# First graph layer rebuilt: paired and merged sorted rows, part of the node rows picked by matmul instead of gathered

## The chip, the cores and the metric

One core of one Trainium2 chip runs the whole kernel. The metric is device time in microseconds (us) from start to end of one execution; lower is better. Engines are named as the profile names them: PE is TensorE (PEld its weight loads), DVE is VectorE, ACT is ScalarE, POOL is GpSimd, SP is SyncE.

## The reference, cut to what matters

```python
N, E, D = 8192, 262144, 128        # nodes, edges, features; dst is sorted, src is random
def layer0(x, src, dst, w, W):     # sums over edges into node src, reads node dst
    pre = segment_sum(x[dst] * w[:, None], src, N)
    return pre @ W.T
def layer1(x, src, dst, attr, ws): # tensor product with 9 attributes, reads src, sums into dst
    return segment_sum(tensor_product(x[src], attr, ws), dst, N) / sqrt(10)
x = layernorm(x + layer0(x, src, dst, edge_weight, W))
x = layernorm(x + layer1(x, src, dst, edge_attr_9, ws))
# dst = floor(8192 * u**2) for uniform u, then sorted; src uniform in 0..8191
```

Only the first layer and its preparation change. Its edges are given in order of dst, but their sums go to src, so both a gather (x[dst]) and a scatter-add (into src) are needed.

## The kernel before, in words

All edges are laid out as 128 rows of 2048, one row per SBUF partition. Five stages follow each other, each in a block of its own, with no overlap between blocks.

**setup** loads src, dst and weight as rows, builds a sort key (dst, and src above it) per edge on DVE, turns rows into columns with 32 PE transposes and ACT copies for the second layer's tables, and clears the accumulator `acc` (features on partitions, nodes along the free axis) on POOL (L220).

**sort_rows** sorts each partition's 2048 keys by src with a merge network of 66 stages on DVE: max, is_gt, min, and two predicated copies that carry the weight (L406 to L414), with ACT copying two halves per stage (L393, L395). Afterwards, element k of every partition has a src near the same place, so a tile of 128 edges, one from each partition, falls in a narrow window of src.

**layer0** loops over 128 rows of 16 tiles (2048 tiles of 128 edges). For each tile POOL gathers 128 rows of x from HBM by an indirect DMA (L525, into `l_feat`, two rows deep, 32 tiles); DVE makes a weighted one-hot of 704 columns (L631: `iota` equals `src_rel`, times `w_row`, eight buffers, `iota` in PSUM); PE multiplies the gathered rows by it in float32, as 512 and 192 columns (L567), adding 16 tiles up in PSUM; then DVE adds the row's 704 columns to `acc` at a window start read from memory (L641). Hand-over is by quads of four tiles: `hot_made` tells PE that four one-hots are there, `quad_done` tells DVE and POOL that PE is done with a quad. Ahead of its first one-hot DVE also makes the tables of the second layer (`layer1_tables`, L588 to L621).

**norm_stage** multiplies the sums by W and normalizes. **layer1** gathers again, 2048 times (L908), makes one-hots of 16 columns times nine attributes, and is not touched by the change; neither is the last **norm_stage**.

What sets the order around the change is the written order on each engine's queue and its semaphore waits; no planner is involved. A few lines of the old loop:

```python
dve.wait_ge(quad_done, u * (R // Q) + (R // Q + q + 3))      # quads up to two back are done
for t in range(Q * q, Q * q + Q):
    last = nc.vector.tensor_scalar(onehot[t % HOTS][:], iota[:, 0:WIN0], g.src_rel[:, col],
                                   g.w_row[:, col], ALU.is_equal, ALU.mult)
last.then_inc(hot_made, 1)
```

## Time and profile before

| what | value |
|---|---|
| median of 3 runs | 6743.53 us (6739.63 to 6747.98) |
| the profiled execution's own time | 6679.32 us |
| its span, first to last instruction | 6677.5 us |
| mean granted TensorE clock | 0.788 of full speed |
| busy: PE, PEld, DVE, ACT, POOL | 4653.5, 3185.8, 3323.1, 513.6, 3885.2 us |
| gathers | 4096, half of them in the first layer |

The profiled execution was shorter than the median of the timed runs by 64 us. Busy time counts compute and the POOL's making of DMA descriptors; register, branch and semaphore instructions are not counted. In the table by stage below, the columns are: stretch and its length in us; busy us (and instructions) of PE, PEld, DVE, ACT and POOL; granted TensorE clock; DMA share; GB/s. In the groups by line, busy us and mean ns stand ahead of the idle time before them and what ended it. A wait put down to "remote" has no releasing instruction in the records (some matmul records are missing).

### The profile page before, as it was taken

The page shows a single profiled execution, that of the slowest core. Times are in us where ns is not written, and L with a number is a line of the kernel's source. Part 1 is how long each engine was busy: PE and PEld are TensorE (multiplying, and loading weights), DVE is VectorE, ACT ScalarE, POOL GpSimd, SP SyncE. Part 2 cuts the span into 40 slices and gives each one's busy share as a digit, 9 for nine tenths or more (in the row PEclk, how much of TensorE's full clock was granted, in tenths as well). Part 3 has the DMA queues.
Part 4 walks back from the last instruction along what each step waited for, and adds up shares of the span by engine and source line. Part 5 has one row for each costly group of instructions (what it writes and reads, how often), then busy time and mean ns, then how long its engine had stood idle before and what let it go on. Part 6 is the DMA issues. An engine that isn't in the chain of part 4 may idle for free. (4 is left out here: it accounts for less than half of the span.)

```text
span 6677.5 us, 67026 instructions
## 1 busy us (share of the span) xinstructions
PE 4653.5 (70%) x16530; PEld 3185.8 (48%) x16531; DVE 3323.1 (50%) x4111; ACT 513.6 (8%) x954; POOL 3885.2 (58%) x4117
## 2 busy tenths in 40 slices
PE   0018888888888888888886666666666666676665
PEld 0004445544444454555455545555555555554454
DVE  9986666666666666666663222222222222222224
ACT  3320000000000000000002000000000000000002
POOL 0026666666666666666654666666666666666663
PEclk5559999999999999999995677776666767656666
DMA  0001111111111111111112111111111111111112
GB/s 22 0 13 44 44 44 44 45 44 44 45 45 44 44 44 45 44 44 45 44 36 83 47 47 47 47 47 47 47 47 47 47 47 47 47 47 47 47 47 78
DMA packets 145732, 298.91 MB, mean 45 GB/s; under 512 B 69280, under 2 KB 69408, under 8 KB 145328
## 3 DMA queue, kind: packets, MB, share of 16 engines
q0 software_dynamic: 131072, 268.70, 15.7%
q1 hardware_dynamic: 10032, 21.62, 1.1%
q10 hardware_dynamic: 4608, 8.39, 0.3%
q14 instruction: 15, 0.12, 0.0%
q8 instruction: 5, 0.08, 0.0%
HBM read 290.04 MB, written 8.39 MB: 45 GB/s over the span
## 5 line engine op out<-in xcount | busy, mean ns | idle before, releaser
L567 PE MATMUL l_pre<-onehot,l_feat 128*128 128x512 f32 (+1 forms) x8192 | 2610.1, 480 | 442.9 <-DVE onehot L631 427.5
L525 POOL DMA_INDIRECT l_feat<-in_x,l_ids x2048 | 1935.1, 945 | 1529.1 <-issue 1059.1
L908 POOL DMA_INDIRECT feat<-x,ids x2048 | 1934.0, 944 | 1124.2 <-issue 584.2
L631 DVE TENSOR_SCALAR onehot<-iota,src_rel,w_row 128x704 f32<-128x704 f32 x2048 | 1918.3, 1004 | 1007.1 <-remote 603.4
L567 PEld LDWEIGHTS l_pre<-onehot,l_feat 128*128 128x128 f32 x8192 | 1510.2, 198 | 1542.5 <-issue 1150.5
L1014 DVE TENSOR_TENSOR group<-group,quad 128x504 f32 (+1 forms) x512 | 347.2, 678 | 2186.0 <-PE quad L972 1115.2
L972 PE MATMUL quad<-attr_hot,feat 128*128 128x144 f32 x4096 | 1000.8, 399 | 559.9 <-issue 558.5
L972 PEld LDWEIGHTS quad<-attr_hot,feat 128*128 128x128 f32 x4096 | 833.6, 275 | 816.7 <-issue 816.1
L979 PE MATMUL mixed<-group,mix 128*128 128x192 f32 x2304 | 649.2, 463 | 333.3 <-DVE group L1014 223.0
L979 PEld LDWEIGHTS mixed<-group,mix 128*128 128x128 f32 x2304 | 607.5, 287 | 368.3 <-DVE group L1014 245.0
L964 PE MATMUL quad<-zero_bf 1*128 1x504 bf16 x512 | 248.6, 486 | 186.7 <-issue 186.4
L1000 DVE TENSOR_TENSOR attr_hot<-hot,attr_t 128x1152 f32<-128x1152 f32 x256 | 346.8, 1355 | 46.7 <-issue 20.2
L457 PE MATMUL turned<-cst,edge 128*128 128x128 f32 x2 | 0.7, 449 | 417.8 <-DVE edge L433 417.8
L549 ACT COPY l_ids<-gather_id 128x8 int32 x256 | 50.5, 197 | 2967.7 <-DMA l_feat<-in_x,l_ids 2943.8
L932 ACT CAST ids<-src_col 128x8 int32 x256 | 50.5, 197 | 2656.9 <-DMA feat<-x,ids 2591.7
L928 ACT ACTIVATE group<-group 128x1728 uint32<-128x1728 uint32 x128 | 210.3, 1643 | 131.5 <-remote 130.2
L457 PEld LDWEIGHTS turned<-cst,edge 128*128 128x128 f32 x2 | 0.3, 204 | 417.9 <-DVE edge L433 417.9
L948 PE MATMUL attr_t<-cst,attr_in 16*128 16x16 f32 x1161 | 154.4, 263 | 14.7 <-DMA attr_in<-in_edge_attr 14.4
L948 PEld LDWEIGHTS attr_t<-cst,attr_in 16*128 16x128 f32 x1161 | 142.0, 203 | 47.6 <-issue 47.6
L964 PEld LDWEIGHTS quad<-zero_bf 1*128 1x128 bf16 x512 | 59.4, 116 | 218.4 <-issue 203.9
L641 DVE TENSOR_TENSOR acc<-acc,l_pre 128x704 f32 x128 | 112.5, 879 | 5.8 <-PE l_pre L567 5.8
L414 DVE COPY_PREDICATED w_row<-swap,w_low 128x512 f32<-128x512 int32 (+9 forms) x66 | 98.0, 1484 | 2.3
(110 smaller groups left out, 904.8 us busy)
## 6 DMA issues: line engine op xcount, KB each, us to landing
l_feat<-in_x,l_ids POOLq DMA_INDIRECT x2048
feat<-x,ids POOLq DMA_INDIRECT x2048
attr_in<-in_edge_attr SPq DMA_DIRECT2D x129, 72.0 KB
norm_x<-in_x SPq DMA_DIRECT2D x16, 256.0 KB, 2.7
x<-norm_z ACTq DMA_DIRECT2D x16, 256.0 KB, 2.4
norm_x<-x SPq DMA_DIRECT2D x16, 256.0 KB, 2.7
out<-norm_z ACTq DMA_DIRECT2D x16, 256.0 KB, 2.4
rows_i<-in_src SPq DMA_DIRECT2D x1, 1024.0 KB, 6.0
```

Of the source, the lines that this page charges most:

```text
L525: pool.indirect_dma_start(feat[z][:, t, :], None, x, bass.IndirectOffsetOnAxis(ap=ids[z][t // H][:, t % H:t % H + 1], axis=0),).then_inc(f ...
L567: last = nc.tensor.matmul(pre[z][:, a:b], feat[z][:, t, :], onehot[t % HOTS][:, a:b], start=(t == 0), stop=(t == R - 1))
L631: last = nc.vector.tensor_scalar(onehot[t % HOTS][:], iota[:, 0:WIN0], g.src_rel[:, col], g.w_row[:, col], ALU.is_equal, ALU.mult)
L641: nc.vector.tensor_tensor(to, to, pre[z][:, 0:WIN0], ALU.add).then_inc(chunk_added, 1)
L908: pool.indirect_dma_start(feat[:, t, :], None, x1, bass.IndirectOffsetOnAxis(ap=ids[t // H][:, t % H:t % H + 1], axis=0),).then_inc(feat_i ...
L928: nc.scalar.memzero(group[z][:]).then_inc(group_zero, 1)
L948: last = nc.tensor.transpose(attr_t[:, z, m * R:(m + 1) * R], edges[:, :, m], g.cst[0:R, C_IDENT:C_IDENT + R])
L964: nc.tensor.matmul(quad[:, q, 0:NA * QUAD_WIN], zero_bf[0:1, 0:P], zero_bf[0:1, :], start=True, stop=False, skip_group_check=True)
L972: nc.tensor.matmul(bank[:, :, bass.ds(off, WIN)], feat[:, t, :], attr_hot[t // H][:, t % H, :, :], start=False, stop=(t % Q == Q - 1), ski ...
L979: last = nc.tensor.matmul(mixed[:, z, 0:GROUP_WIN], g.mix[:, m, :], group[z][:, m, :], start=(m == 0), stop=(m == NA - 1))
L1000: nc.vector.tensor_tensor(attr_hot[h][:], hot[:].unsqueeze(2).to_broadcast(s4), by_tile[:, h * H:h * H + H, :].unsqueeze(3).to_broadcast(s ...
L1014: nc.vector.tensor_tensor(to, to, quad[:, q, 0:NA * QUAD_WIN].rearrange("p (m n) -> p m n", m=NA), ALU.add).then_inc(quad_added, 1)
```

## The change

Rows r and 127-r are put on neighbouring partitions ("lanes" of a pair; `C_ROW`, `C_TURN`). With dst spread as the square of u, such a pair always covers about 128 different values of dst. Each lane is sorted as before, one of the two with its sign turned; the two lanes are then merged: they are exchanged by DMA (`far_keys`, `far_w`), compared once over 2048 elements, and run through four further stages (`blocks`). Now each pair holds 4096 edges in order of src, in 32 tiles of 128 edges that lie along the free axis; weights, dst and relative src are turned into columns by 48 PE transposes and 24 ACT copies.

A tile is now one pair's, so its src window is 360 columns (not 704), and its dst are within 160 nodes. Tiles are worked in groups of eight (256 groups). Of each eight, five are gathered (`GATHERS`) and three are picked (`FETCHED`): the pair's 160 nodes of x lie in SBUF, 128 of them split into three bfloat16 parts (`x_near`), the other 32 as three parts on spare partitions (`x_rest`). PE spreads the dst positions (`spread`, 3 bfloat16 matmuls a group), ACT and DVE make two 128-column one-hots a tile from them (`rest`, `near`), and PE picks the rows in four bfloat16 matmuls a tile (`fetch`); ACT copies them to SBUF (`message`). All eight tiles then go through one float32 matmul of 360 columns each into a PSUM window at an address read from memory (`pe_places`), 64 tiles added up in three banks, which DVE adds to `acc` (`adds`, 3 times 512 columns in every eight groups). POOL makes `x_near` and `x_rest` in six batches (8 gathers, 8 small operations each) beside the sort. The one-hots' `iota` is now in SBUF (it was in PSUM), the one-hot buffers are 16, the gather buffers 20. The rows of setup are loaded by three indirect DMAs on POOL, ahead of the clearing of `acc`; the tables of the second layer move from layer0 into setup.

The diff, cut to its core:

```diff
-WIN0 = 704
+WIN0 = 360
+BANKS = 3
+STEP = 512 - WIN0
+GROUP = 8
+FETCHED = (0, 3, 6)
+GATHERS = (1, 2, 4, 5, 7)
+KIND = (0, 2, 1, 0, 2, 1, 0, 1)
+FEATS = 20
+SUMMED0 = 18
+SPAN = 160
...
         def _(pool):                                    # setup
+            pool.wait_ge(row_no_made, 1)
+            pool.sem_inc(pool_turn, 1)
+            for k, (to, row) in enumerate(((rows_i[0], src), (rows_i[1], dst), (g.w_row, weight))):
+                pool.indirect_dma_start(to[:], None, row.rearrange("(r c) -> r c", r=RN),
+                                        bass.IndirectOffsetOnAxis(ap=row_no[:], axis=0)).then_inc(rows_in[k], 16)
             nc.gpsimd.memset(g.acc[:], 0.0)
...
+            link(nc.vector.tensor_reduce(lanes[:, 0, 0:1], rows_f[1][:], AX_X, ALU.min))
+            link(nc.vector.tensor_reduce(lanes[:, 0, 1:2], rows_f[1][:], AX_X, ALU.max))
...
+            layer1_tables(dve)
...
+    blocks = [(d, d) for d in (n // 2, n // 4, n // 8, P)]
...
+                if s == n_sort:
+                    dve.sem_inc(lanes_sorted, 1)
+                    dve.wait_ge(far_in, 64)
+                    nc.vector.scalar_tensor_tensor(swap[:], far_keys[:], -1.0, g.keys[:], ALU.mult,
+                                                   ALU.is_lt).then_inc(compared, 1)
+                    dve.wait_ge(compared, s + 1)
+                    nc.vector.scalar_tensor_tensor(g.keys[:], far_keys[:], -1.0, g.keys[:], ALU.mult, ALU.min)
+                    nc.vector.copy_predicated(g.w_row[:], swap[:], far_w[:]).then_inc(merged, 1)
...
+            def near(k, z):                              # DVE
+                dve.wait_ge(copied, k + 2)
+                dve.wait_ge(got_made, k + 1)
+                nc.vector.tensor_scalar(near_hot[z][:], place[z][:], wanted, None, ALU.is_equal).then_inc(near_made, 1)
+            def hots(k, h, s, j):
+                dve.wait_ge(staged, h * 3 + 3)
+                dve.wait_ge(summed, k * 2 + (SUMMED0 - 2))
+                for i in range(GROUP):
+                    c = j * GROUP + i
+                    made = nc.vector.tensor_scalar(hot_of[(j % 2) * GROUP + i], iota[KIND[i]], src_of[s][:, c:c + 1],
+                                                   w_of[s][:, c:c + 1], ALU.is_equal, ALU.mult)
+                    if i % 4 == 3:
+                        made.then_inc(hot_made, 1)
...
+            def rest(k, z):                              # ACT
+                act.wait_ge(placed, k + 1)
+                act.wait_ge(near_made, k + 1)
+                nc.scalar.copy(place[z][:], place_b[:, 0:NF * P]).then_inc(copied, 1)
...
+                nc.scalar.activation(rest_far[:], place[z][:], ACT.Abs, bias=not_wanted).then_inc(far_made, 1)
+                act.wait_ge(far_made, k + 1)
+                act.wait_ge(got_made, k + 1)
+                nc.scalar.activation(rest_hot[z][:], rest_far[:], ACT.Relu, bias=1.0, scale=-1.0).then_inc(rest_made, 1)
+            def message(k, z):
+                act.wait_ge(got_made, k + 3)
+                act.wait_ge(summed, k * 2 + (SUMMED0 - 2))
+                nc.scalar.copy(msg[z][:].rearrange("p a b -> p (a b)"), got[:, 0:NF * P]).then_inc(msg_made, 1)
...
+            for b in range(BATCHES):                     # POOL, beside the sort
+                for c, rows, landed in ((1, rest_in, rest_here), (0, near_rows, near_in)):
+                    for i in range(GATHERED):
+                        pool.indirect_dma_start(rows[:, i, :], None, x, ...).then_inc(landed, 16)
+                nc.gpsimd.tensor_copy(part, rest_in[:]).then_inc(pool_split, 1)
+                nc.gpsimd.tensor_tensor(rest_left[:], rest_in[:], part, ALU.subtract).then_inc(pool_split, 1)
...
+                                pool.wait_ge(summed, k * 2 + (SUMMED0 - 2 * (FEATS // NG) + 2))
+                                for m, i in enumerate(GATHERS):
+                                    pool.indirect_dma_start(feat[:, slot, :], None, x, ...).then_inc(feat_in[slot], 16)
...
+            def fetch(k, j):                             # PE
+                pe.wait_ge(near_made, k + 3)
+                pe.wait_ge(rest_made, k + 3)
+                pe.wait_ge(msg_made, k + 1)
+                for m in range(NF):
+                    for part in range(3):
+                        nc.tensor.matmul(to, near_hot[z][:, m * P:(m + 1) * P], x_near[:, a, part, :],
+                                         start=(part == 0), stop=False)
+                    last = nc.tensor.matmul(to, rest_hot[z][:, m * P:(m + 1) * P], x_rest[:, a, :], start=False,
+                                            stop=True)
+                last.then_inc(got_made, 1)
+            def sums(k, w, t, s, j):
+                places = pe_places(t, s, j)              # eight window starts read into registers
...
+                    made = nc.tensor.matmul(pre[:, s, bass.ds(places[i], WIN0)], rows, hot_of[(j % 2) * GROUP + i],
+                                            start=False, stop=(j == GROUPS - 1 and i == GROUP - 1),
+                                            skip_group_check=True)
+                    if i % 4 == 3:
+                        made.then_inc(summed, 1)
...
+                    def slots(t, final):                 # PE's order, group by group
+                                    spread(k + 2, ...)
+                                    fetch(k + 1, (j + 1) % GROUPS)
+                                sums(k, w, t, s, j)
```

The diff's calls are shortened where `...` stands inside a line, and `slots` is shown without its loop heads. DVE's order per group is near(k+2), hots(k+1), and in one group of eight adds; ACT's is rest(k+2), message(k+1).

## Rows read from the trace of the kernel before

**Rows 1.** Page, part 1: busy us and share of the span, whole kernel.
```profile
PE 4653.5 (70%) x16530; PEld 3185.8 (48%) x16531; DVE 3323.1 (50%) x4111; ACT 513.6 (8%) x954; POOL 3885.2 (58%) x4117
```

**Rows 2.** Busy time by stage: sort, layer0, layer1.
```profile
31.00:457.00 426.00, 1.70 (x6) 1.22 (x6) 408.64 (x350) 128.97 (x137) 0.00 (x0) 0.50 0.00 0
457.00:3504.00 3047.00, 2609.83 (x8192) 1510.23 (x8192) 2027.26 (x2190) 50.55 (x256) 1935.11 (x2048) 0.95 0.17 44
...
3563.00:6604.00 3041.00, 1966.44 (x8026) 1612.99 (x8027) 782.60 (x1145) 259.80 (x383) 1930.19 (x2044) 0.68 0.18 47
```

**Rows 3.** Groups of instructions by line, 457 to 3504 us (layer0).
```profile
L567 PE MATMUL l_pre<-onehot,l_feat 128*128 128x512 f32 (+1 forms) x8192 | 2610.1, 480 | 442.9 <-DVE onehot L631 427.5 <-issue 14.7
L525 POOL DMA_INDIRECT l_feat<-in_x,l_ids x2048 | 1935.1, 945 | 1529.1 <-issue 1059.1 <-PE l_pre L567 248.1 <-remote 221.9
```

**Rows 4.** Timeline of POOL in mid layer0: start, us, instruction, [idle before it].
```profile
2022.58 0.94 POOL L525 DMA_INDIRECT l_feat<-in_x,l_ids  x1 [3.06 <-PE l_pre L567]
```

**Rows 5.** Timeline of POOL while DVE makes the second layer's tables.
```profile
469.51 1.18 POOL L525 DMA_INDIRECT l_feat<-in_x,l_ids  x1 [0.30 <-issue]
...
472.25 1.38 POOL L525 DMA_INDIRECT l_feat<-in_x,l_ids  x1 [0.30 <-issue]
473.93 2.72 POOL L525 DMA_INDIRECT l_feat<-in_x,l_ids  x1 [0.30 <-issue]
```

**Rows 6.** Timeline of DVE at the end of layer0, when the gathers are over.
```profile
3485.46 3.77 DVE L631 TENSOR_SCALAR onehot<-iota,src_rel,w_row 128x704 f32<-128x704 f32 x4 [0.97 <-PE l_pre L567]
...
3490.19 3.77 DVE L631 TENSOR_SCALAR onehot<-iota,src_rel,w_row 128x704 f32<-128x704 f32 x4 [0.17 <-PE l_pre L567]
```

**Rows 7.** Timeline of DVE, the tables of the second layer, to its first one-hots.
```profile
463.98 0.46 DVE L588 TENSOR_TENSOR mix<-w_scalar,cst 128x288 f32<-128x288 f32 x1 [9.26 <-issue]
...
465.39 1.75 DVE L612 TENSOR_TENSOR off_f<-tile_start 128x1536 f32<-128x1536 f32 x1
...
469.40 0.48 DVE L607 TENSOR_SCALAR tile_offs<-word_f,keep 128x512 int32<-128x512 f32 x1
469.92 1.07 DVE L615 TENSOR_TENSOR off_f<-tile_start 128x512 f32<-128x512 f32 x1
...
472.19 1.32 DVE L618 TENSOR_SCALAR off_f<-tile_start,keep 128x2048 f32<-128x2048 f32 x1
473.54 2.29 DVE L619 TENSOR_TENSOR dst_rel<-dst_col,off_f 128x2048 f32<-128x2048 f32 x1
...
477.45 2.85 DVE L631 TENSOR_SCALAR onehot<-iota,src_rel,w_row 128x704 f32<-128x704 f32 x3 [1.18 <-issue]
```

**Rows 8.** Timeline of DVE in mid layer0, at the same place as POOL's.
```profile
2021.93 7.44 DVE L631 TENSOR_SCALAR onehot<-iota,src_rel,w_row 128x704 f32<-128x704 f32 x8 [5.00 <-remote]
```

**Rows 9.** Timeline of PE in setup: bfloat16 matmuls of 128 columns.
```profile
20.06 0.22 PE L299 MATMUL pt<-ident_bf,dst_lo 128*128 128x128 bf16 x1
20.11 0.22 PE L299 MATMUL pt<-ident_bf,dst_hi 128*128 128x128 bf16 x1
```

**Rows 10.** Timeline of a late sort stage, what follows the sort, ACT's 704 columns.
```profile
425.06 1.23 DVE L412 COPY_PREDICATED w_row<-swap,w_row 128x1020 f32<-128x1020 int32 x1
...
444.71 1.16 DVE L428 TENSOR_SCALAR src_i<-keys 128x2048 int32<-128x2048 int32 x1
...
455.07 0.75 ACT L537 COPY iota<-cst 128x704 f32<-128x704 f32 x1 [14.04 <-PEq L343]
```

**Rows 11.** Timeline of setup: clearing of acc, first cast of rows, a wait for ACT.
```profile
0.75 7.51 POOL L220 MEMSET acc<- 128x8896 f32 x1 [0.29 <-POOLq L1065]
...
7.64 1.76 DVE L236 CAST rows_f<-rows_i 128x2048 f32<-128x2048 int32 x1
...
24.28 0.18 DVE L263 COPY src_col<-src_col 128x16 f32<-128x16 f32 x1 [3.14 <-ACT tile_start L319]
```

**Rows 12.** Page, part 6: the load of the weights: count, KB, us to landing.
```profile
w_row<-in_edge_weight SPq DMA_DIRECT2D x1, 1024.0 KB, 10.0
```

**Rows 13.** Page, part 5: PE weight load behind a window start read from memory (layer1).
```profile
L964 PEld LDWEIGHTS quad<-zero_bf 1*128 1x128 bf16 x512 | 59.4, 116 | 218.4 <-issue 203.9
```

More of the change, by code:

```diff
@@ L165, in set_passes, with setup @@
     nc.vector.tensor_scalar(g.n_pass[:, layer:layer + 1], on, float(passes - 1), 1.0, ALU.mult, ALU.add)
-def setup(nc, g, src, dst, weight, w_lin, consts):
+def setup(nc, g, src, dst, weight, w_lin, w_tp, consts):
     RN, TN = g.RN, g.TN
@@ L188, in setup @@
         some = sb("some", [P, 4], F32)
+        g.tile_start = sb("tile_start", [P, TN], F32)
+        row_no = sb("row_no", [P, 1], I32)
+        turn_bf = sb("turn_bf", [P, P], BF16)
+        lanes = sb("lanes", [P, 2, 2], F32)
+        extent = sb("extent", [P, 2], F32)
+        lower = sb("lower", [P, 2], F32)
+        upper = sb("upper", [P, 2], F32)
+        keep_a = sb("keep_a", [P, 1], F32)
+        shown_in = sb("shown_in", [P, 3, PAIRS], F32)
+        w_scalar = sb("w_scalar", [P, MUL], F32)
+        w_vec = [sb(f"w_vec{i}", [P, MUL], F32) for i in range(2)]
+        off_f = sb("off_f", [P, TN], F32)
+        word_f = sb("word_f", [P, TN // QUAD_TILES], F32)
         some1 = sb("some1", [P, 1], F32)
@@ new lines, in _ @@
+            link(nc.vector.scalar_tensor_tensor(lower[:], lower[:], g.cst[:, C_UPPER:C_UPPER + 1], own,
+                                                ALU.mult, ALU.add))
+            link(nc.vector.tensor_tensor(upper[:], own, other, ALU.add))
+            link(nc.vector.tensor_tensor(upper[:], upper[:], lower[:], ALU.subtract))
+            link(nc.vector.tensor_tensor(extent[:, 1:2], lower[:, 1:2], upper[:, 0:1], ALU.subtract))
+            link(nc.vector.tensor_scalar(extent[:, 1:2], extent[:, 1:2], 0.5, None, ALU.is_gt))
@@ new lines, in _ @@
+            dve.wait_ge(miss_sum, 1)
+            link(nc.vector.tensor_scalar(some[:], pa[:, 0, 0:4], 0.5, None, ALU.is_gt))
+            link(nc.vector.tensor_reduce(some1[:], some[:, 1:4], AX_X, ALU.max))
+            set_passes(nc, g, 1, WIN, g.PASSES1, some1[:])
+            nc.vector.tensor_copy(g.on[:, 0:1], some[:, 0:1])
+            link(nc.vector.tensor_scalar(keep_a[:], some[:, 0:1], -1.0, 1.0, ALU.mult, ALU.add))
+            nc.vector.tensor_copy(g.pair[:, 1:2], upper[:, 0:1])
+            link(nc.vector.tensor_tensor(g.pair[:, 0:1], lower[:, 0:1], keep_a[:], ALU.mult))
@@ new lines, in _ @@
+            link(nc.vector.tensor_tensor(g.pair[:, 2:3], upper[:, 0:1], lower[:, 1:2], ALU.subtract))
+            link(nc.vector.tensor_scalar(g.pair[:, 2:3], g.pair[:, 2:3], 1.0, keep_a[:], ALU.subtract, ALU.mult))
+            link(nc.vector.tensor_tensor(g.pair[:, 3:4], lower[:, 1:2], lower[:, 0:1], ALU.subtract))
+            link(nc.vector.tensor_scalar(g.pair[:, 3:4], g.pair[:, 3:4], 1.0, None, ALU.add))
+            for k, col in enumerate((3, 0, 2)):
+                link(nc.vector.tensor_scalar(shown_in[:, k, :], g.cst[:, C_IDENT:C_IDENT + P:2],
+                                             g.pair[:, col:col + 1], None, ALU.mult))
@@ new lines, in _ @@
+        @block.scalar
+        def _(act):
+            cols = [g.src_col, g.dst_col]
+            for n in range(n_groups):
+                if n < len(col_groups):
+                    which, q = col_groups[n]
+                    dest = cols[which]
+                else:
+                    q, dest = n - len(col_groups), g.tile_start
+                act.wait_ge(group_done, n + 1)
+                o = dest[:, 0:TN].rearrange("p (r k) -> p k r", k=ROW_TILES)[:, 4 * q:4 * q + 4, :]
+                i = pt[:, n % 4, :].rearrange("p (j r) -> p j r", j=4)[:, :, 0:RN]
+                nc.scalar.copy(o, i).then_inc(group_out, 1)
+            act.wait_ge(wt_done, 1)
+            nc.scalar.copy(g.w_t[:], pa[:, 1, 0:P])
```

987 lines of the change are left out of this document (629 added, 358 removed).

## The prediction, made before the changed kernel was run

> **What bounds the kernel now.** I read the busy shares first [rows 1]: no engine is above 70%, so no engine bounds the whole. The table by stage [rows 2] says more: the span is a preparation of 457 us, layer0 of 3047 us, a norm to 3563, layer1 of 3041 us and a last norm. The preparation is DVE's (409 of 426 us busy in the sort). layer0 has PE 86% busy at a granted clock of 0.95, almost all of it the upper level, 2.4 GHz, after a sort at 0.50, 1.2 GHz, in which PE did nothing. layer1 has 2044 gathers in 3041 us and isn't touched; I leave its time as it is.
>
> Next, the groups of layer0 [rows 3]. PE idles 443 us, 428 of them until one-hots come; DVE idles 3047 - 2027 = 1020 us [rows 2], POOL 248 + 222 = 470 us besides its issue gaps. Each waits for the others. Their floors: POOL needs 0.94 + 0.30 = 1.25 us a gather (they start that far apart) [rows 4, 5], 16 x 1.25 = 20.0 us a row of tiles, 2560 us in all. PE, when gathers are long over and DVE follows it step by step, starts a quad every 3490.19 - 3485.46 = 4.73 us [rows 6], 18.9 us a row. Real pace: from the first one-hot at 477.45 [rows 7] to the end at 3504 is 3027 us with the last addition, 23.6 us a row, 1.18 times POOL's floor and 1.25 times PE's. The excess is hand-over: DVE stands 5.0 us ahead of eight one-hots, until a release that the records don't show [rows 8], and POOL 3.06 us until PE frees its buffer, at nearly the same moment [rows 4].
>
> The chain of waits that the page shows reaches back only through the last norm, so I go by the stages.
>
> **The loop after, per group of eight tiles (256 groups).**
>
> POOL: five gathers, 5 x 1.25 = 6.25 us, 1600 us in all, against 2560.
>
> PE: 704 columns took 4.73 / 4 = 1.18 us, so 360 take 0.605 us, and eight 4.84 us. The pick adds 3 + 12 bfloat16 matmuls of 128 columns with their weight loads; the rows show such pairs 0.055 us apart at the upper clock [rows 9]: 0.83 us. Three clearing matmuls in eight groups add about 0.1. Sum 5.8 us, 1480 us in all.
>
> DVE: a 704-column one-hot comes every 3.77 / 4 = 0.94 us [rows 6]. One column costs (2.29 - 1.75) / 512 = 1.05 ns [rows 7], so 360 columns take 0.94 - 0.36 = 0.58 us at this rate. But `iota` moves from PSUM to SBUF, and a one-source float32 operation from SBUF ran at double rate: 2048 elements in 1.32 us against 2.29 us for two sources [rows 7]. That takes 0.19 off: 0.39 us. I take 0.39 (0.58 is the bound). Eight are 3.15 us, `near` over 384 columns at most 0.48 [rows 7], I take 0.35, and three additions of 512 columns at 0.69 (2.29 less 1536 columns) in eight groups 0.26: 3.8 us (5.3 at the slow rate). DVE is covered by POOL either way.
>
> ACT: three operations over 384 columns and a copy of 384, each below the 0.75 us of 704 columns [rows 10]: under 3 us, covered too.
>
> What isn't free is DVE's double rate. Beside the tables the gathers got longer [rows 5]: 1.18 us beside a 0.48 us operation, 1.38 beside the 1.32 us one, 2.72 beside a two-source one of 2.29 us. The first of these ended 0.82 us after the DVE operation (469.88 to 470.69), the last also (475.83 to 476.65); the middle one ended 0.12 us after it. So I read a gather as two short accesses, near its start and at its end, each of which may have to wait for the DVE operation of the moment, and can slip in between two. With operations of 0.39 to 0.44 us an access waits at most that, half on the mean, and 3.5 of some 7 us of a group are such operations: 5 gathers x 2 x 0.2 x 0.5 = 1 us at most; I take 0.65, so POOL needs 6.9 us. Bounds: 0 and all of 3.5.
>
> The Trainium skill, SBUF — State Buffer, "Who interferes with whom", says that such a DVE operation holds the port pair that GpSimd needs for its whole length and that the other blocks fully. The middle and last gathers agree, but no row shows a train of such operations, where the question is who gets in between; if nobody does, the sum is 9.75 us a group instead of 7.4, the rival below.
>
> Pace: the old loop ran 1.18 times the floor of its slowest engine. 6.25 x 1.18 = 7.4; with 6.9 as the floor that leaves 0.5 for hand-over, less than before, but each hand-over is now per eight tiles, not four, and POOL is four groups ahead. I take 7.4 us: 256 x 7.4 = 1894 us, and 6.6 to 8.2 as this case's own range. PE is then busy 5.8 of 7.4 us in short gaps, 78%, between layer0's 86% at clock 0.95 and layer1's 65% at 0.68 [rows 2]. I take the upper level; at the lower level everywhere the matmuls would take 11.6 us, but PE would then never stop.
>
> **The preparation after.**
>
> Setup. The clearing of `acc` (7.51 us, from 0.75 [rows 11]) now follows three gathers that wait for the constants: I put their start at 5.0, so it runs from 5.0 + 3 x 1.25 = 8.75 to 16.3. The first cast of rows (7.64 to 9.40) is a double-rate one and gets its data at about 9.7 (the gathers start later than the plain loads did), so it ends behind the clearing, at 17.6: +8.2. Two reductions of 2048, at the 2.29 of [rows 7], and twelve small dependent steps, which I put at 0.2, are 7.0, of which 3.1 lie in a wait that DVE has for ACT [rows 11]: +3.9. Steps for the pairs: 8 x 0.2 + 3 x 0.29 = 2.5, nodes 1.6. The tables move here with 463.98 to 476.3 = 12.3 us. Sum +28.5.
>
> Sort. Four more stages, all with long runs: 3 x 1.21 + 2 x 1.23 [rows 10] = 6.1 each, 24.5. The merge: sign 1.3, exchange of 2 MB about 10 (an estimate from the three 1 MB loads of setup, the last of which landed after 10.0 us [rows 12]), two two-source operations 4.6, predicated copy 2.5: 18.4.
>
> POOL beside the sort. 48 gathers (60 us) and 48 operations of up to 512 columns are hidden in 470 us, but hold up two-source DVE operations, which fill the sort. If each of the 48 costs DVE its length, 0.54 us for a one-source one by the slope above and, as a bound, twice that for a two-source one, that is 40 us; I take 20 (bounds 0 and 45). The Trainium skill, GPSIMD Engine Reference, 3.1, gives 2.6 cycles at 1.2 GHz per element for two sources, thus 1.1 us for 512; no run here shows it.
>
> After the sort. Before, the first operation behind the sort, at 444.71 [rows 10], was 32.7 us ahead of the first one-hot. After: five operations at double rate 6.1, two reductions 4.6, some 25 small steps 6, the subtraction 2.3, the last four transposes with their ACT copies 5.6, then `iota` 1.5, staging, gathers, spread and first one-hots 8: 34 with rounding, the small ones my estimate. +1.
>
> First one-hot at 477.45 + 28.5 + 24.5 + 18.4 + 20 + 1 = 570. Loop to 2464, last additions to 2468, against about 3505. 1037 us gone: span 5640, time 5642. The profiled execution lay at 6679.3 beside a median of 6743.5; I keep the ratio 1.0096: **5697 us**.
>
> **The rivals.** Each us per group is worth 256 us, 258 in the median.
>
> *As forecast*, pace 6.6 to 8.2: 5490 to 5905. Chance 0.62.
>
> *The gathers are locked out of the whole train*: 6.25 + 3.5 = 9.75 us, +602: 6304. For: the 2.72 us gather. Against: the first gather of [rows 5] went on at 469.87, between two operations 0.04 us apart [rows 7]. 0.11.
>
> *PE's sequencer*: `pe_places` reads eight window starts per group. In layer1 each weight load behind such a read idles 218.4 / 512 = 0.43 us [rows 13]. Eight in a row uncovered: 5.8 + 3.4 = 9.2 us, +465: 6160; with the queue ahead of the array nothing. 0.11.
>
> *Better*: hand-overs vanish and DVE slips by, 6.4 us, sort undisturbed: -276 in the span: 5418. 0.10.
>
> *Slower than before*: the pick's chain isn't hidden by its one group of lead. Spread 0.17, ACT copy, abs and relu 0.75 each, fetch 0.66, message 0.75, sums 4.84 are 8.7 us, and if a release by PE comes late as in [rows 8], 4 us more: 12.7 us a group, 1357 us over the forecast: 7067. It decides from 7.4 + 1037 / 256 = 11.4 us on. Against it: the chain starts a whole group ahead. 0.05. The windows themselves hold for the reference's inputs: worked out from them, a tile spans at most 328 nodes of the 360, a pair's dst 134 of the 158 allowed, so one pass is enough; I give a second pass under 0.01.
>
> **How the numbers follow.** 0.62 + 0.10 + 0.11 + 0.11 = 0.94 is faster, the slower case 0.05, and 0.01 is left for no change. Within 0.2%, 13 us, is about what a measurement of this kernel can't tell from no change. The range leaves out the slower case, most of the lock-out and half of the better case: 5440 to 6200.
>
> **What would show it.** 1280 + 48 + 3 gathers outside layer1; one-hots of 360 columns every 0.39 us; gathers of 0.94 us alone and 1.1 to 1.4 beside them; bfloat16 matmuls 0.055 us apart; PE idle below 2 us per group; first one-hots near 570 us, first norm near 2470; layer1 3041 us as before. Wrong if: gathers over 1.6 us on the mean (lock-out); PE idle ahead of the first sum of each group with nothing late (sequencer); PE or ACT waiting for each other in each group (chain); sort stages longer than 6.3 us on the mean; granted clock below 0.9 in the loop.

## The result, and the profile after

The changed kernel took 5838.48 us (median of 4 runs, 5833.05 to 5846.71) where the kernel before took 6741.58: a ratio of 0.866 (95% interval 0.8645 to 0.8675). The forecast was 5697, range 5440 to 6200. The miss of 141 us is the difference of two larger errors: the profiled span is 5836.6, 197 us above the forecast 5640, and the factor 1.0096 between profile and median, which I had carried over, was 1.0003 this time, 55 us less.

The page after, busy shares and granted clock (compare [rows 1]):

```profile
PE 3670.6 (63%) x16451; PEld 2712.9 (46%) x16452; DVE 2323.7 (40%) x4418; ACT 1009.3 (17%) x1845; POOL 3423.7 (59%) x3448
...
PEclk6555999999999999996666676676676676666676
```

Busy time by stage: the sort, layer0, layer1 (compare [rows 2]). Columns: length, then each engine's busy time with its instructions, granted clock, DMA share, GB/s.

```profile
core 0: us, PE busy (x) PEld busy (x) DVE busy (x) ACT busy (x) POOL busy (x), PEclk, DMA share, GB/s
31.00:503.60 472.60, 5.83 (x39) 4.95 (x39) 454.32 (x397) 131.37 (x137) 153.18 (x96) 0.50 0.02 7
574.00:2632.00 2058.00, 1627.58 (x8024) 1039.11 (x8022) 934.78 (x2399) 528.86 (x1113) 1316.99 (x1279) 0.96 0.14 41
2688.00:5783.00 3095.00, 1962.61 (x8073) 1607.21 (x8073) 782.96 (x1154) 259.84 (x384) 1933.39 (x2048) 0.68 0.16 46
```

The loop takes 2058 us instead of 1898: 164 us of the 197 lie ahead of 2632 (4 of them before the first one-hot), the other 33 behind it, in a stage that the change doesn't touch. PE is busy 79% of the loop. The groups of the loop (compare [rows 3]):

```profile
L960 POOL DMA_INDIRECT l_feat<-in_x,id_of x1279 | 1317.0, 1030 | 722.3 <-issue 397.6 <-PE l_pre L1045 276.1 <-remote 48.5
...
L1045 PE MATMUL l_pre<-keys,msg 128*128 128x360 f32 x512 | 234.8, 544 | 164.8 <-issue 121.9 <-ACT msg L692 40.3 <-DVE pad L844 2.6
L1045 PE MATMUL l_pre<-w_row,msg 128*128 128x360 f32 x512 | 212.2, 497 | 206.7 <-issue 129.9 <-ACT msg L692 68.9 <-DVE keys L844 8.0
```

POOL waits 276 us for PE, so it isn't what sets the pace. PE's idle time is nearly all at one spot: 164.8 + 206.7 = 371.5 us ahead of the first sum of 224 groups (the other 32 begin with the clearing matmuls), 1.66 us each, 252 us of it with no releaser ("issue"), 109 put down to ACT's copy `message` (`msg`). That name is a rival to test: in a second profile of the same kernel (after_again, below) 334 of 339 us of this idle time carry it. One group in the timeline (the rows between left out):

```profile
2560.81 0.87 PE L1045 MATMUL l_pre<-keys,msg 128*128 128x360 f32 x2 [1.46 <-issue]
...
2565.75 0.33 PE L1002 MATMUL place_b<-pos,ident_bf 128*128 128x128 bf16 x3
...
2566.53 0.22 PE L1019 MATMUL got<-x_rest,rest_hot 128*128 128x128 bf16 x1
2568.15 0.87 PE L1045 MATMUL l_pre<-w_row,msg 128*128 128x360 f32 x2 [1.40 <-issue]
...
2569.03 0.99 POOL L960 DMA_INDIRECT l_feat<-in_x,id_of  x1 [2.28 <-remote]
```

The spread starts at 2565.75, right behind the sums; it and the fetch take 1.0 us (the matmuls 0.055 apart), and then PE stands still for 1.4 us. What its queue did meanwhile shows the line of `pe_places`, in this group's stretch 2564 to 2568.2 (columns: shortest, median, longest in ns, first and last start):

```profile
L1054 PEldq FUSED_REGOPS  x8: 146/146/151, 2565.5 to 2567.5; - x8
L1054 PEldq SEQ_ASSERT  x8: 18/18/18, 2565.7 to 2567.7; - x8
L1054 PEldq TENSOR_LOAD <-starts_row x1: 592/592/592, 2564.9 to 2564.9; - x1
```

A load of 0.59 us, then eight times a register operation and a bound's check, 0.28 us a pair: 2.9 us, begun only 0.9 us before the spread, ended 1.0 us after the last fetch. Spread to spread, the median group takes 7.46 us.

### The profile page after: what moved, and what is told of

Read it like the earlier page. It is cut to its first block and busy times, and to the rows that moved or that the text cites. A ratio compares the mean times of both kernels' runs of the same rounds, so it can differ in the third digit from the quotient of the medians.

```text
span 5836.6 us, 72428 instructions
## 1 busy us (share of the span) xinstructions
PE 3670.6 (63%) x16451; PEld 2712.9 (46%) x16452; DVE 2323.7 (40%) x4418; ACT 1009.3 (17%) x1845; POOL 3423.7 (59%) x3448
## 5 line engine op out<-in xcount | busy, mean ns | idle before, releaser
L960 POOL DMA_INDIRECT l_feat<-in_x,id_of x1280 | 1318.0, 1030 | 1056.9 <-issue 397.6
L1045 PE MATMUL l_pre<-w_row,msg 128*128 128x360 f32 x512 | 212.2, 497 | 206.7 <-issue 129.9
L680 ACT CAST place<-place_b 128x384 bf16<-128x384 f32 x256 | 122.4, 478 | 1250.8 <-PE place_b L1002 740.5
L1045 PE MATMUL l_pre<-keys,msg 128*128 128x360 f32 x512 | 234.8, 544 | 164.8 <-issue 121.9
L1045 PE MATMUL l_pre<-keys,l_feat 128*128 128x360 f32 x768 | 316.1, 526 | 0.0
L1045 PE MATMUL l_pre<-w_row,l_feat 128*128 128x360 f32 x768 | 299.0, 471 | 0.0
L1045 PE MATMUL l_pre<-pad,l_feat 128*128 128x360 f32 x768 | 279.2, 473 | 0.0
L844 DVE TENSOR_SCALAR w_row<-swap,src_of,w_of 128x360 f32<-128x360 f32 x640 | 266.1, 464 | 1.3 <-PE l_pre L1045 1.1
L844 DVE TENSOR_SCALAR keys<-swap,src_of,w_of 128x360 f32<-128x360 f32 x640 | 256.7, 465 | 0.6 <-issue 0.3
L844 DVE TENSOR_SCALAR pad<-swap,src_of,w_of 128x360 f32<-128x360 f32 x640 | 250.9, 456 | 0.0
```

The costliest lines, as they stand in the source:

```text
L680: nc.scalar.copy(place[z][:], place_b[:, 0:NF * P]).then_inc(copied, 1)
L844: made = nc.vector.tensor_scalar(hot_of[(j % 2) * GROUP + i], iota[KIND[i]], src_of[s][:, c:c + 1], w_of[s][:, c:c + 1], ALU.is_equal, ALU ...
L960: pool.indirect_dma_start(feat[:, slot, :], None, x, bass.IndirectOffsetOnAxis(ap=id_of[s][:, c:c + 1], axis=0)).then_inc(feat_in[slot], 16)
L1045: made = nc.tensor.matmul(pre[:, s, bass.ds(places[i], WIN0)], rows, hot_of[(j % 2) * GROUP + i], start=False, stop=(j == GROUPS - 1 and i ...
```

## Experiments

The chips differ: the kernel before took 6742 us in the first comparison, and 5707, 5708, 6759 and 6682 us in the four calls of the experiments. So times are compared within a call, or between calls with the same time before. "Pace" is the mean (median) time in us from one group's first spread to the next in the profiled execution; the granted clock is that of the loop from 620 us on.

| kernel | before | this | ratio (95%) | pace | clock |
|---|---|---|---|---|---|
| changed, first result | 6741.6 | 5838.5 | 0.866 (0.8645-0.8675) | 8.03 (7.46) | 0.96 |
| places_const | 5706.7 | 4967.9 | 0.8703 (0.8688-0.8717) | 6.68 (6.68) | 1.00 |
| places_halves | 5706.7 | 4971.3 | 0.8709 (0.8695-0.8724) | 6.70 (6.63) | 0.99 |
| places_first | 5706.7 | 4978.1 | 0.8722 (0.8707-0.8736) | 6.72 (6.75) | 1.00 |
| near_f32 | 5706.7 | 4974.6 | 0.8715 (0.8701-0.873) | 6.75 (6.57) | 1.00 |
| after_again | 5707.5 | 5220.1 | 0.9149 (0.9134-0.9165) | 7.67 (7.46) | 0.98 |
| f32_halves | 5707.5 | 4969.4 | 0.8707 (0.8692-0.8721) | 6.73 (6.67) | 1.00 |
| halves_odd | 5707.5 | 4970.2 | 0.871 (0.8695-0.8724) | 6.68 (6.63) | 0.99 |
| f32_six_more | 6758.7 | 6472.9 | 0.9577 (0.9561-0.9593) | 10.52 (10.31) | 0.82 |
| thin_hots | 6758.7 | 5872.6 | 0.8686 (0.8672-0.8701) | 8.15 (7.59) | 0.91 |
| four_picked | 6758.7 | 5554.8 | 0.8218 (0.8204-0.8231) | 6.87 (6.01) | 0.97 |
| four_reads_back | 6681.9 | 6392.6 | 0.9567 (0.9551-0.9583) | 10.30 (10.18) | 0.83 |

**1. No reads (places_const).** This kernel leaves the window starts out and sums into fixed columns.

```
-                places = pe_places(t, s, j)
+                places = [(i % BANKS) * 512 for i in range(GROUP)]
```

> PE no longer reads the eight window starts of a group: the sums go to fixed columns, so its output is not the reference's. Theory A (the reads are what PE waits for): in the changed kernel the first sum of a group starts 1.5 to 1.7 us after the last pick, in each group. Without the reads that gap falls under 0.3 us, PE needs 5.9 us a group, and POOL becomes the slowest with 5 gathers of 1.03 + 0.30 = 6.65 us: 256 x (7.46 - 6.7) = 195 us less. The 40 stretches at the lower clock, 3.4 us each, which follow such gaps, go too: up to another 105 us. In all 5540 to 5650 us. Theory B (the gap is the wait for ACT's copy of the picked rows, or for a late release by PE): the gap stays at 1.5 us and the time at 5838 within 20 us.

**2 and 3. The same reads elsewhere (places_halves, places_first).** `places_first` moves the call ahead of `spread`; `places_halves` reads four there and four within the sums:

```
+    places = pe_places(t, s, j, 0)
     spread(k + 2, ...)
     fetch(k + 1, ...)
     sums(k, w, t, s, j, places)
...
+    if i == GROUP // 2:
+        places = places + pe_places(t, s, j, 1)
```

> The same reads, the same result, at other places of PE's stream: four of them ahead of the spread, four in the middle of the sums. Theory A: each four take 4 x 0.28 + 0.6 = 1.7 us of the sequencer, and it runs about 2.4 us ahead of the array there, so all are covered and the kernel comes within 30 us of the one without reads: 5550 to 5680 us. Theory B: no change, 5838 within 20 us. If the sequencer isn't as far ahead as that, a gap of up to 1.5 us shows up in the middle of the sums, and the time stays near 5840.

> All eight reads ahead of the spread and the fetch instead of behind them, the same result. They take 8 x 0.28 + 0.6 = 2.85 us, and the sequencer is done with the sums about 2.4 us ahead of the array: theory A says a gap of some 0.5 us ahead of the spread in place of 1.5 to 1.7 behind it, 256 x 0.8 to 1.0 = 205 to 250 us less, down to POOL's pace, and most of the low-clock stretches gone: 5560 to 5700 us. Theory B: no change, 5838 within 20 us.

**4. The larger pick as one float32 product (near_f32).**

```
-    for part in range(3):
-        nc.tensor.matmul(to, near_hot[z][...], x_near[:, a, part, :], start=(part == 0), stop=False)
+    nc.tensor.matmul(to, near_hot[z][...], x_near[:, a, :], start=True, stop=False)
```

`x_near` and `near_hot` are float32, the rows are gathered straight into `x_near`, and the four POOL operations of `near_split` go.

> Undoes the last step alone: the larger pick as one float32 product with its rows gathered straight into place, so POOL has 24 of its 48 operations beside the sort, and PE one float32 product in place of three bfloat16 ones per picked tile. PE: a float32 product of 128 columns should take 0.605 x 128 / 360 = 0.22 us against 3 x 0.055 = 0.17, or up to 0.30 if its weight load sets it: 3 x 0.05 to 0.13 = 0.15 to 0.4 us more a group, 40 to 100 us, if PE and its sequencer follow one another as theory A has it (the reads overlap more with a longer fetch, so then as little as 0). Sort: with half of POOL's operations gone, about half of the 28 us that it grew by come back, 10 to 17 us. Sum 5820 to 5925 us. Under theory B a longer fetch adds in full: 5860 to 5925.

**5. The changed kernel and the kernel before once more (after_again, before_again).**

> The changed kernel once more, unchanged, on the chip of this call, as a measure for the others: the kernel before ran in 5707 us on the chip of the earlier experiments and in 6742 us on the chip of the first comparison. Theory A (the reads are what PE waits for, and it is POOL that hides what lies under 6.7 us a group): with the gap of 1.5 us at full length in each group, 7.46 us a group and about 5160 us where the kernel without reads took 4968. If the kernel without reads gained nothing, it is 4970 within 15 us, and the gap belongs to the first chip, not to the kernel.

> The kernel before, unchanged, with a profile on the chip of this call, to read its stages beside those of the others. On the first chip layer0 took 3047 us and layer1 3041 us of a span of 6677. If the chip of the earlier experiments is met again (5707 us), layer1 should take the 2580 us that it takes in their traces, and layer0 about 5705 - 457 - 60 - 55 - 2580 = 2550 us, 19.9 us a row: POOL's floor of 20.0 that the prediction worked out, with no hand-over on top.

The time before is the same in these two calls (5706.7, 5707.5), so their kernels can be set side by side. Against after_again's 5220.1, leaving the reads out gives 252 us, and reading the same values elsewhere 249 or 242: theory A, not B. These edits leave ACT's copy where it is, so the copy isn't the cause, though the page of after_again names it:

```profile
L1045 PE MATMUL l_pre<-w_row,msg 128*128 128x360 f32 x512 | 209.3, 491 | 193.7 <-ACT msg L692 192.3
L1045 PE MATMUL l_pre<-keys,msg 128*128 128x360 f32 x512 | 222.1, 517 | 144.9 <-ACT msg L692 142.1
```

after_again was expected at about 5160; the 60 us more are mostly groups with a stretch at the lower clock (below). The times expected of the other three were too high because of the chips: layer1 alone is 528 us shorter here than in the first profile, and the changed kernel's loop 92 us. The gap behind the fetch is gone from the timeline of places_halves, its sums follow the last fetch at once:

```profile
1502.02 0.34 PE L1002 MATMUL place_b<-pos,ident_bf 128*128 x3 [0.69 <-issue]
...
1502.96 0.22 PE L1019 MATMUL got<-x_rest,rest_hot 128*128 128x128 bf16 x1
1503.02 0.82 PE L1046 MATMUL l_pre<-keys,msg 128*128 128x360 f32 x2
```

The reads aren't quite free there either: the 0.69 us ahead of the spread end with the first half's reads (at 1501.97). Such a stop has a median of 0.55 us in places_halves and of 0.60 us in places_first, where some 0.5 was expected; POOL's pace hides it. What is left sets that pace: POOL, whose gaps in places_halves are issue alone (from 620 us to 2270), 5 x (1.035 + 0.30) = 6.68 us.

```profile
L960 POOL DMA_INDIRECT l_feat<-in_x,id_of x1232 | 1275.7, 1035 | 375.5 <-issue 373.6 <-PE l_pre L1046 1.8
```

near_f32 leaves the reads where they are and still takes 4974.6, 245 us less than the changed kernel. I had expected it slower, or 18 us faster at best. Its fetch is 0.3 us longer, and its reads begin at 1502.6, 1.4 us before the spread instead of 0.9. The timeline of near_f32:

```profile
1503.95 0.33 PE L989 MATMUL place_b<-pos,ident_bf 128*128 x3
...
1505.06 0.22 PE L1004 MATMUL got<-x_rest,rest_hot 128*128 128x128 bf16 x1
1505.90 0.87 PE L1030 MATMUL l_pre<-w_row,msg 128*128 128x360 f32 x2 [0.62 <-issue]
```

The stop is 0.6 us in this group, where it was 1.4 (median of all groups 0.3 instead of 1.5), and the median group takes 6.57 us. Its first `near` is at 560.2 instead of 572.4: half of POOL's operations beside the sort gone, 12 us back, as expected (10 to 17). The other 233 of the 245 us are the loop's.

before_again, by stage, and under it after_again:

```profile
477.00:3028.00 2551.00, 2523.01 (x8192) 1434.31 (x8192) 2032.45 (x2180) 50.35 (x255) 1922.14 (x2036) 1.00 0.20 52
3085.00:5655.00 2570.00, 1963.79 (x8081) 1490.53 (x8081) 799.28 (x1156) 257.93 (x385) 1932.89 (x2048) 0.75 0.21 56
```

```profile
574.00:2540.00 1966.00, 1581.71 (x8025) 1017.84 (x8022) 945.93 (x2399) 519.43 (x1113) 1308.82 (x1279) 0.98 0.16 43
2594.00:5166.00 2572.00, 1970.50 (x8081) 1495.44 (x8081) 793.75 (x1156) 258.12 (x386) 1933.72 (x2048) 0.75 0.21 56
```

layer1 takes 2570 us on this chip in both kernels, where it took 3041 us in the first profile of before and 3095 in that of the changed kernel. layer0 of before ran at 19.9 us a row, POOL's floor of 20.0 from the prediction, with nothing on top: the factor 1.18 that I took for hand-over belongs to the chip of that first profile.

**6. Three edits together (f32_halves).** near_f32 with the reads in halves and `acc` cleared ahead of the gathers of the rows.

> Three edits together, same result: the larger pick as one float32 product (half of POOL's operations beside the sort gone), the window starts read in two halves, and the clearing of acc started at once instead of behind the gathers of the rows. Where the earlier experiments ran (before at 5707): the loop is POOL's, 5 gathers of 1.03 + 0.30 = 6.65 us a group, so the reads give nothing beyond near_f32's 4975; the start shrinks by 5 to 8 us through the clearing: 4965 to 4972, ratio to before 0.870 to 0.8715. Where before takes 6742: the gap goes, ratio 0.82 to 0.85.

4969.4, POOL's pace again. The time lies in the expected range, but not for the reason given: of the 5 to 8 us from the early clearing nothing came (the first `near` is at 560.3, in near_f32 at 560.2), and the 5 us less than near_f32 are the loop's. The changed kernel on the first chip:

```profile
8.88 7.62 POOL L281 MEMSET acc<- 128x9008 f32 x1
11.01 7.70 DVE L348 CAST rows_f<-rows_i 128x2048 f32<-128x2048 int32 x2 [6.34 <-DMA rows_i<-in_src,row_no]
```

and f32_halves:

```profile
14.04 1.23 DVE L348 CAST rows_f<-rows_i 128x2048 f32<-128x2048 int32 x1 [5.49 <-DMA rows_i<-in_src,row_no]
17.55 1.23 DVE L348 CAST rows_f<-rows_i 128x2048 f32<-128x2048 int32 x1 [2.29 <-DMA rows_i<-in_dst,row_no]
```

The clearing did hold up the casts, as forecast, but behind it the gathered rows land one after the other, 3.5 us apart, and end the casts at the same 18.8 us.

**7. One-hots of odd width (halves_odd).** 359 columns in the one-hots and the sums.

> The reads in two halves as in places_halves, and one-hots and sums 359 instead of 360 columns wide (no window of the inputs is wider than 328 nodes, so the result is the same). If an odd width ends DVE's double rate, a one-hot takes 0.39 x 2 - 0.2 = 0.58 us, the train of eight 4.6 us, and if gathers are lengthened by the double rate alone they come back from 1.03 to 0.94 us: 5 x 0.09 = 0.45 us a group, 115 us less where POOL sets the pace (ratio to before 0.85 where places_halves had 0.871). If the width changes nothing in DVE's rate, no change in either. If gathers wait for any operation of DVE on SBUF, they get longer with its operations: up to 5 x 2 x 0.1 = 1 us a group more, ratio up to 0.91.

A one-hot still takes 0.46 us, 0.38 apart; neither rate nor time moved, so this says nothing on the gathers.

```profile
L844 DVE TENSOR_SCALAR w_row<-swap,src_of,w_of 128x359 f32<-128x359 f32 x621 | 258.1, 464 | 2.5 <-PE l_pre L1046 2.3
```

**8. More matmuls in PE's queue (f32_six_more).** near_f32 with, ahead of the fetch:

```
+    for m in range(2 * NF):
+        nc.tensor.matmul(got[:, NF * P:NF * P + 8], zero_bf[0:1, 0:P], zero_bf[0:1, 0:8], start=True, stop=True)
```

> near_f32 with six small bfloat16 matmuls more per group (one row, eight columns, into an unused corner of got, same result), so that PE's stream has 15 matmuls between the sums and the reads again, as in the changed kernel, instead of 9. The array's own work for them is at most 6 x 0.055 = 0.33 us. Theory Q (what counts is how many matmuls stand in PE's queue: the sequencer reaches the reads only as the sums drain, 1.5 to 1.8 us later with 15 entries than with 9): the first sum starts about 2.4 us after the last spread again, the loop goes back to about 7.4 to 7.8 us a group and the time to 5180 to 5300 where near_f32 took 4975. Theory L (it is the greater length of the float32 product, 3 x 0.17 us, that covers the reads, not the count): the six cost nothing that POOL's pace of 6.7 us doesn't hide, 4975 to 4990.

6473 us, 10.3 us a group: theory L is out. Theory Q's wait came, but its time was too low: 7.4 to 7.8 us a group were expected (a ratio of 0.91 to 0.93), since it left out the clock. Beside near_f32's 6.6 us, six matmuls that keep the array busy for 0.3 us go with 3.7 us more a group, 1.6 of them PE's longer standstill, most of the rest the lower clock. near_f32 itself was not run on this slower chip. But the chip hardly disturbs this kernel's loop: 5 of its register operations take over 0.3 us, where the changed kernel's first profile has 114, and its eight reads have their usual length. A float32 product is two passes in the trace, so 18 passes now stand between the sums and the reads. In one group whose spread began at 1500.54, the queue's rows read:

```profile
L1042 PEldq FUSED_REGOPS  x9: 51/146/151, 1500.8 to 1503.6; - x9
L1042 PEldq SEQ_ASSERT  x8: 18/18/18, 1501.8 to 1503.8; - x8
L1042 PEldq TENSOR_LOAD <-starts_row x1: 591/591/591, 1500.9 to 1500.9; - x1
```

The reads began 0.4 us after the spread; PE then stood still for 1.8 us, and for 2.0 on the mean of all groups. After each such stop the sums ran at the lower clock for a while, which the changed kernel shows in some groups only, here 1282.4 to 1285.8 of its first profile, with the granted clock of that stretch (0.50 is 1.2 GHz):

```profile
1281.69 0.90 PE L1045 MATMUL l_pre<-keys,msg 128*128 128x360 f32 x2 [2.31 <-issue]
...
1282.40 2.59 PE L1045 MATMUL l_pre<-keys,l_feat 128*128 128x360 f32 x4
```

```profile
1282.50:1285.80 3.30, 3.30 (x7) 1.91 (x6) 1.17 (x4) 0.00 (x0) 2.63 (x3) 0.50 0.13 41
```

The passes of the sums stand 0.60 instead of 0.30 us apart there, and the group takes 9.7 to 9.9 us. The trace's clock record has 42 stretches at the lower level in the changed kernel's loop (first to last spread) on the first chip, 22 in after_again, 253 in f32_six_more, 249 in four_reads_back, 6 in places_halves, 1 in places_const (each with those at the loop's start). On the slower chips kernels without a stop behind the fetch have them too: 84 in thin_hots, 20 in four_picked.

**9. One-hots of 8 columns (thin_hots).** places_halves with `[:, 0:8]` in the one-hots; the rest of each is left out.

> places_halves with one-hots of 8 columns in place of 360 (the rest of each keeps older values, so the output is not the reference's): the same instructions, waits and sums, but DVE's train is 8 operations of some 0.06 us instead of 0.46. If the train is what lengthens the gathers, they fall from 1.035 to 0.94 us on the mean, POOL from 6.7 to 5 x 1.25 = 6.25 us a group, and the kernel from 4971 to 4855 to 4890 (PE needs about 6.0 and lets it). If the gathers keep their 1.03, the lengthening isn't the train's: 4960 to 4975.

```profile
L960 POOL DMA_INDIRECT l_feat<-in_x,id_of x1195 | 1130.6, 946 | 809.5 <-issue 338.9 <-PE l_pre L1046 292.8 <-remote 177.8
```

The gathers fell from 1035 to 946 ns: the train lengthens them, by 0.09 us each, 0.45 a group. The time is another matter: expected was 4855 to 4890 where before takes 5707, a ratio of 0.851 to 0.857, and measured 0.869, no better than the changed kernel's 0.866. This call's chip is a slow one. With POOL's brake gone PE runs groups of 5.73 us, the forecast's 5.8, and then others of 10 us; 515 of its register operations in the loop take over 0.3 us, up to 1.44 (none in places_halves), and 111 of ACT's 256 copies of picked rows start over 2 us after the fetch that they wait for (none in places_halves). This is also the only kernel with moved reads and five gathers that ran on a slow chip: what places_halves gains there isn't shown.

**10. Four picked, four gathered (four_picked).** places_halves with:

```
-FETCHED = (0, 3, 6)
-GATHERS = (1, 2, 4, 5, 7)
-KIND = (0, 2, 1, 0, 2, 1, 0, 1)
-FEATS = 20
+FETCHED = (0, 2, 4, 6)
+GATHERS = (1, 3, 5, 7)
+KIND = (0, 1, 0, 1, 0, 1, 0, 1)
+FEATS = 8
```

`near_left` shares `rest_left`'s room.

> places_halves with four picked and four gathered tiles of each eight instead of three and five, same result; two ring slots' worth of groups for the gathers instead of four, for room. POOL then needs 4 x 1.33 = 5.3 us a group, PE 5.8 + 0.28 = 6.1 to 6.3 us, and becomes the slowest, if the sequencer's lead still covers its reads (19 matmuls stand between the sums now): 256 x (6.7 - 6.2) = 130 us less than 4971, and some 10 us more beside the sort, where POOL has 64 gathers and 64 operations instead of 48 and 48: 4840 to 4890. If the four extra matmuls use up the lead, a gap of 0.3 to 1 us ahead of the sums takes it all back: 4920 to 5050.

5554.8, ratio 0.8218 (0.8204 to 0.8231), against the changed kernel's 0.866 on a chip of the same sort: the best version. The expected 4840 to 4890 us would be a ratio of 0.848 to 0.857 on the chip of 5707. The median group is 6.01 us, just under PE's expected 6.1 to 6.3; POOL waits for PE (369 us), and the stop ahead of the spread has a median of 0.

**11. The same with the reads back (four_reads_back).**

```
-    places = pe_places(t, s, j, 0)      # ahead of the spread
-        places = places + pe_places(t, s, j, 1)
+    places = pe_places(t, s, j)         # in sums, behind the fetch
```

> four_picked with the eight reads back where the changed kernel has them, between the last pick and the first sum, same result. POOL's floor is 5.3 us and the array's own work 6.1 us a group, so by the engines' loads it should be as fast as four_picked. Theory Q (PE reaches the reads only as its queue of matmuls drains, and the queue is longer by four here than in the changed kernel): PE stands still 1.6 to 2.0 us ahead of the sums of each group, 7.7 to 8.1 us a group, and if the lower clock follows each such stop, as in f32_six_more, up to 10.3. Against four_picked that is 256 x 1.6 = 410 to 256 x 4.2 = 1075 us more: 5960 to 6630 on a chip where before takes 6759 (ratio 0.88 to 0.98), 5260 to 5900 where it takes 5707 (0.92 to 1.03). It should thus be slower than the changed kernel, though POOL has a fifth less to do. If the loads decide, its ratio is four_picked's 0.82 to 0.85.

0.9567, in the upper part of theory Q's 0.88 to 0.98: 10.2 us a group, 2.3 of them PE's stop. With less gathering than the changed kernel it is far slower than it, 0.957 against 0.866. None of its register operations in the loop takes over 0.2 us, so the long register operations of the slow chips aren't the cause. Its timeline:

```profile
1507.35 0.22 PE L1020 MATMUL got<-x_rest,rest_hot 128*128 128x128 bf16 x1
1509.86 0.87 PE L1046 MATMUL l_pre<-w_row,msg 128*128 128x360 f32 x2 [2.29 <-DVE keys L844]
```

The releaser named is misleading: DVE's one-hots of the next group were being made from 1507.6 on, while PE's queue was reading until 1509.4.

## Why the prediction came out as it did

**Forecast right for a wrong reason: 7.4 us a group.** The median is 7.46. But the prediction had it as POOL's 6.9 and 0.5 of hand-over. POOL's true 6.65 is reached with no hand-over at all (6.68 without reads), and the 7.46, the same on the first chip and on that of after_again, is PE's: its own work of some 5.9 and a stop of 1.5. The step that failed is "with the queue ahead of the array nothing" against "eight in a row uncovered": I gave the rival 0.11 and only its full price, 9.2 us. The truth lies between: 2.9 us of reads (the rival had 3.4), of which PE's queue and the fetch covered half. The chance should have been spread over what part is covered, and asked at what point of the program the sequencer comes to the reads. Of the prediction's own signs of being wrong two came true: "PE idle ahead of the first sum of each group with nothing late", and sort stages longer than 6.3 us on the mean (6.7). That the total lay so near the forecast is luck: a hand-over that isn't there stood in for a stop that is.

**The change's last step.** I priced three bfloat16 products in place of one by the array, 0.055 us each, and that held. Its real price lies in the queue: 15 passes instead of 12 between sums and reads, and a shorter fetch to cover them. near_f32 undoes it and gains 245 us (0.8715 against 0.9149), 12 of them beside the sort. With the reads moved, the two forms are equal (4971.3, 4969.4): POOL hides either (in the profiles the float32 form begins its loop 12 us earlier and takes 6 us longer for it).

**The clock.** I took the upper level throughout. The loop's mean exceeds its median by 0.57 us, 147 us over 255 groups: 22 in two groups at the very start, and 125 in 56 later ones, 40 of them with a stretch at 1.2 GHz. That is most of the loop's miss of 160; the pace itself is 15. Part of it is the kernel's: in after_again mean less median is 0.21 us, 54 us in all, in 28 groups at every eighth place, and the kernels without the stop have hardly any low stretch on such a chip. The other 93 us are the first chip's: 56 of them in 27 long groups at other places, nearly all with a stop of 1.9 to 2.8 us. In one of them, the group whose slow stretch from 1282.4 on is shown above, the reads begin together with the spread (at 1278.4) instead of 0.8 us before it: PE's sequencer comes later still. Why it does on this chip isn't shown.

**layer1.** "As before" failed by 33 us on the first chip, with the same instructions. This goes with the chip and not with the change. From norm0's first load to norm1's the profiles have:

| kernel | before took, in that call | us |
|---|---|---|
| before_again and the seven others of its two chips | 5707, 5708 | 2622.0 to 2622.9 |
| four_reads_back | 6682 | 3116.1 |
| changed, first result | 6742 | 3150.4 |
| thin_hots, four_picked, f32_six_more | 6759 | 3154.5 to 3158.1 |
| before, its own time 6679.3 | | 3116.7 |

The profile of before fits the chip of 6682, the timed runs beside the changed kernel a slower one. That accounts for the 33 us, and for the ratio 1.0096 that I carried over: 6743.5 and 6679.3 are then two chips' times. No profile of before on the chip of 6742 exists to close this. In the changed kernel's profile the register operations at `pe_places` took up to 1079 ns on the first chip and at most 173 in after_again:

```profile
L1054 PEldq FUSED_REGOPS  x2288: 2/146/1079, 575.8 to 2623.4; - x191
L1054 PEldq SEQ_ASSERT  x2048: 2/18/702, 576.9 to 2623.6; - x187
```

```profile
L1054 PEldq FUSED_REGOPS  x2288: 46/146/173, 575.9 to 2531.4; - x191
L1054 PEldq SEQ_ASSERT  x2048: 18/18/18, 576.9 to 2531.6; - x187
```

The same holds for the operations of PE's sequencer in layer1: 236 to 343 of 0.65 to 0.8 us in each profile from a chip whose time before was 6682 to 6759, none where it was 5707. Why those chips' PE does this isn't settled.

**The terms that held.** PE's work: 5.8, measured 5.73 in its densest groups. One-hots: 0.39 apart by forecast, 0.38 measured (five in 1.97 us). Gathers: the lock was taken as 0.65 us a group and measured at 0.45, so the lock-out rival (9.75) is dead: beside a train of eight operations back to back the gathers took 0.09 us more on average, 99 of 100 in after_again at most 0.26 us more. The Trainium skill, SBUF — State Buffer, "Who interferes with whom", has the port held for an operation's length and the other blocked; within one operation that fits, between two of a train 0.38 us apart the gathers got in. First one-hots: 574.15 against 570, near it because errors cancel: the sort's growth beside POOL was 27 us (441 for 66 stages where it was 414) instead of 20, setup about 2 us more, the merge 3 and what follows the sort 2 us less. POOL's two-source operations of 512 columns took 1.37 to 3.01 us each beside DVE's sort. The Trainium skill, GPSIMD Engine Reference, 3.1, gives about 2.6 cycles an element for two sources, from which 1.1 us is an estimate; the trace has more in each of them, but with DVE at work beside them, so it doesn't settle the page's figure. The merge cost 15.1 us instead of 18.4 (503.6 to 517.5 and the sign's 1.2), the four stages 6.3 each instead of 6.1. The clearing of `acc`, which I blamed for 8.2 us, was only one of two things late at that spot (f32_halves).

## What to carry to other kernels

Register reads on PE are free only as far as its queue is ahead of its array, and how far that is depends on what stands queued between. Here the reads behind the long float32 sums cost nothing in the time, with POOL setting the pace, and the same reads behind 15 short passes cost 1.5 us a group. Splitting them in two was worth 7 us more. When a product is replaced by several cheaper ones, count entries in the queue as well as columns. A pace that comes out as forecast proves no step of the forecast: the edit that leaves the suspected cost out does. It also decides where the profile names another releaser, as it named ACT's copy here. And a profile and the times that it is set beside should come from one chip.

## What was not expected of the hardware

- PE's standstills cost twice: in the changed kernel, with a median stop of 1.5 us a group, the lower clock came in one group of six (first chip) or of twelve (after_again); in f32_six_more, with 2.0 on the mean, in nearly each (253 stretches for 256 groups). In the changed kernel such a group takes about 2.3 us longer.
- The same program takes 5707 us on two chips and 6682 to 6759 on others; layer1 alone, from norm to norm, 2622 against 3116 to 3158. On the slower ones single register operations of PE take 0.7 us instead of 0.02 to 0.15, and in the changed kernel ACT's copies of picked rows start over 2 us after their fetch in 123 of 256 groups (none in after_again).
- Six matmuls of one row and eight columns, 0.3 us of array time, went with a group of 10.3 us instead of 6.6 (on two different chips; the reads moved back did the same, 10.2 in four_reads_back against four_picked's 6.0, both on slow ones).
